# A DLRM tower on one core: gathers paced by the one two back, each with its own semaphore

## What is computed

```python
e = jnp.stack([tbl_0[ids[:, 0]], ..., tbl_25[ids[:, 25]]], axis=1)
combined = jnp.concatenate([dense_features[:, None, :], e], axis=1)        # 512 x 27 x 128
interactions = jnp.einsum('bfd,bgd->bfg', combined, combined)
z = jnp.concatenate([dense_features, interactions[:, iu, ju]], axis=1)    # iu, ju: upper triangle
h = jnp.concatenate([z, dense_features], axis=1)                          # 607 columns
h = jnp.maximum(h @ W_top1 + b_top1, 0.0)                                 # 512
h = jnp.maximum(h @ W_top2 + b_top2, 0.0)                                 # 256
y = h @ W_top3                                                            # 512 x 1
```

## Time and profile before

| | us |
|---|---|
| median of 3 runs | 160.23 |
| lowest and highest run | 157.64 and 160.42 |
| the profiled execution's own time | 156.5 |
| its span, from the first to the last instruction | 154.7 |

### The profile page before, as it was taken

One profiled execution on the slowest core, in us unless ns is written; L12 is line 12 of the kernel. 1 busy time (PEld: TensorE's weight loads), 2 busy tenths in 40 slices (PEclk: granted clock), 3 DMA queues, 4 the chain that ended last, 5 costly groups with the idle time before them and its releaser, 6 DMA issues.

```text
span 154.7 us, 2685 instructions
## 1 busy us (share of the span) xinstructions
PE 117.9 (76%) x1038; PEld 98.9 (64%) x1038; DVE 74.1 (48%) x153; ACT 73.0 (47%) x160; POOL 68.4 (44%) x75
## 2 busy tenths in 40 slices
PE   0689999985979967550595728489929989799994
PEld 0446776662756856540394628478829989798993
DVE  3499999999999960407204510030505020237000
ACT  6795994995897820426104522002505313236211
POOL 2648072260345747474447465446456474100000
PEclk9999999999999999776559997865985799999999
DMA  5828765487961011111112121111121111100000
GB/s 156 222 71 267 207 190 110 160 221 199 354 181 42 17 51 38 34 51 34 39 44 52 28 63 32 49 34 38 34 51 33 39 50 25 27 6 0 4 0 1
DMA packets 6304, 12.58 MB, mean 81 GB/s; under 512 B 2545, under 2 KB 3157, under 8 KB 6163
## 3 DMA queue, kind: packets, MB, share of 16 engines
q1 hardware_dynamic: 3971, 7.68, 17.2%
q0 software_dynamic: 2176, 4.46, 10.9%
q10 hardware_dynamic: 144, 0.26, 0.8%
HBM read 11.27 MB, written 0.00 MB: 73 GB/s over the span
## 4 chain that ended last, share of the span: by engine, by line
DMA 34%; PE 27%; POOL 24%; issue 13%; DVE 1%; ACT 1%
DMA rows<-in_tbl_dram,ids_i 31%; POOL rows L343 24%; PE ps L603 12%; PE ps L574 7%; PE ps L525 2%; PE ps L616 2%; DMA ids_i<-in_ids_dram 2%; PE ps L558 2%; DVE z L488 1%; PE ps L626 1%; PE ps L624 1%; ACT emb_t L403 0%; DVE h_t L497 0%; ACT y L430 0%
## 5 line engine op out<-in xcount | busy, mean ns | idle before, releaser
L343 POOL DMA_INDIRECT rows<-in_tbl_dram,ids_i x68 | 67.6, 994 | 63.0 <-DMA rows<-in_tbl_dram,ids_i 45.2
L461 DVE TENSOR_SCALAR hot<-ps,row_no 125x512 fp32r<-125x512 f32 x54 | 36.6, 739 | 1.0 <-PE ps L512 1.0
L488 DVE COPY z<-ps 32x112 f32<-32x112 f32 (+1 forms) x64 | 16.5, 258 | 34.9 <-PE ps L574 22.7
L574 PE MATMUL ps<-emb_t 128*64 128x52 f32 x512 | 23.6, 251 | 11.8 <-issue 8.3
L574 PEld LDWEIGHTS ps<-emb_t 128*64 128x64 f32 x512 | 21.1, 166 | 14.8 <-issue 11.3
L542 PE MATMUL ps<-hot,tab_hi 125*128 125x512 f32 x72 | 30.0, 416 | 0.8 <-issue 0.8
L411 ACT COPY z<-ps 32x112 f32<-32x112 f32 (+1 forms) x64 | 15.2, 238 | 30.8 <-PE ps L574 19.7
L545 PE MATMUL ps<-hot,tab_lo 125*128 125x512 f32 x72 | 29.1, 404 | 0.7 <-DVE tab_lo L450 0.7
L558 PE MATMUL ps<-ident,rows 128*128 128x128 f32 x68 | 12.0, 304 | 15.2 <-DMA rows<-in_tbl_dram,ids_i 9.7
L558 PEld LDWEIGHTS ps<-ident,rows 128*128 128x128 f32 x68 | 8.3, 153 | 18.3 <-DMA rows<-in_tbl_dram,ids_i 11.7
L542 PEld LDWEIGHTS ps<-hot,tab_hi 125*128 125x128 f32 x72 | 14.1, 196 | 5.5 <-issue 2.4
(11 more groups left out here) (44 smaller groups left out, 92.7 us busy)
## 6 DMA issues: line engine op xcount, KB each, us to landing
tab<-in_tbl_dram SPq DMA_DIRECT2D x9, 448.0 KB
rows<-in_tbl_dram,ids_i POOLq DMA_INDIRECT x68, 4.6
w_fold<-w_pair SPq DMA_DIRECT2D x1, 1024.0 KB
w<-in_W_top_dram SPq DMA_DIRECT2D x1, 512.0 KB, 5.1
tab<-in_tbl_dram SPq DMA_DIRECT2D x9, 52.0 KB
x_rows<-in_r_dense_features_dram ACTq DMA_DIRECT2D x1, 256.0 KB, 3.2
w_x<-in_W_top_dram SPq DMA_DIRECT2D x1, 256.0 KB
h_t<-in_W_top_dram SPq DMA_DIRECT2D x1, 256.0 KB
```

The costliest lines, as they stand in the source:

```text
L343: pool.indirect_dma_start(out=rows[:, t, gathered.index(f), :], out_offset=None, in_=tables[f - 1], in_offset=bass.IndirectOffsetOnAxis(id ...
L461: nc.vector.tensor_scalar(hot[0:RP, k % OHB], ps[0:RP, IDV + n % 2, :], row_no[0:RP, c:c + 1], None, ALU.is_equal).then_inc(hot_dve, 1)
L488: last = nc.vector.tensor_copy(dst, src)
L574: last = nc.tensor.matmul(ps[32 * q:32 * (q + GT), bank, col:col + GC], emb_t[:, t, b0:b0 + GT, :].rearrange("p b f -> p (b f)"), emb_t[:, ...
```

## The change

POOL no longer waits for a whole group ahead of the next. From the third gather on, each gather waits for the one two back, so that at most two are under way at any time. Each of the 68 gathers gets a semaphore of its own (before there were 20, one per group). PE's transposes wait for the gather that each of them reads, in place of one wait for the group ahead of the first. The wait for the PSUM bank stands ahead of them as before. Nothing else changes: the same 68 gathers in the same order, the same `ORDER`.

```diff
-        rows_in = [[sem(f"rows_in{t}_{g}") for g in range(NG)] for t in range(T)]
+        rows_in = [[sem(f"rows_in{t}_{f}") for f in gathered] for t in range(T)]
...
             pool.wait_ge(ids_in, 16)
+            fetched = []
             for t in range(T):
-                for g, group in enumerate(GROUPS):
-                    fetched = [f for f in features(group) if f]
-                    for n, f in enumerate(fetched):
-
-                        if n == 0 and g:
-                            pool.wait_ge(rows_in[t][g - 1], 16 * sum(a > 0 for a in features(GROUPS[g - 1])))
-                        elif n == 0 and t:
-                            pool.wait_ge(rows_in[t - 1][NG - 1], 16 * len(features(GROUPS[NG - 1])))
-                        pool.indirect_dma_start(
-                            out=rows[:, t, gathered.index(f), :], out_offset=None, in_=tables[f - 1],
-                            in_offset=bass.IndirectOffsetOnAxis(ids_i[:, t, f - 1:f], 0),
-                        ).then_inc(rows_in[t][g], 16)
+                for group in GROUPS:
+                    for f in features(group):
+                        if f:
+
+                            if len(fetched) >= 2:
+                                pool.wait_ge(fetched[-2], 16)
+                            landed = rows_in[t][gathered.index(f)]
+                            pool.indirect_dma_start(
+                                out=rows[:, t, gathered.index(f), :], out_offset=None, in_=tables[f - 1],
+                                in_offset=bass.IndirectOffsetOnAxis(ids_i[:, t, f - 1:f], 0),
+                            ).then_inc(landed, 16)
+                            fetched.append(landed)
...
-                    pe.wait_ge(rows_in[t][g], 16 * (len(feats) - (0 in feats)))
                     wait_bank(s)
                     for m, f in enumerate(feats):
+                        if f:
+                            pe.wait_ge(rows_in[t][gathered.index(f)], 16)
```

## The result

The changed kernel took 148.46 us (median of 4 runs, 146.66 to 151.37) against 158.95 us (median of 4, 157.64 to 160.42) for the kernel before, which has one run more here than in the table ahead (160.23): a ratio of 0.938, 95% interval 0.922 to 0.954. It is faster, by some 10 us; 151.4 was forecast, which is 150.1 when the 8.85 us are taken from 158.95. The profiled execution took 146.66 us with a span of 144.9, against 156.5 and 154.7 before, so 9.8 us of span are to be explained.

The account below looks back on a forecast made before the run. Gathers were taken to bound the kernel up to 104.02 us, PE the last 50.7. Removing PE's four waits (6.85) plus 2 us extra gave 8.85 off 160.2, so 151.4 us; range 146 to 158.

Parts of the forecast that it names:

- the likeliest case: Whole kernel: the forecast itself, a gain of 5.5 to 11 us, chance 0.58.
- The pace without loads: POOL's gathers in tiles 1 and 2: 1.40 us each, 34 in 49.8 us with slow rows, before 60.04.
- The pace beside loads: POOL's gathers up to 44 us, beside table loads: 2.33 to 3.00 us each with two under way, before 2.43.
- I take 43.4, in effect no change: Tile 0, beside table loads: the 17th gather lands at 43.4 us, before 43.94.
- Rival A: Table loads hold up the early gathers, the 17th landing at 48.7: time 156 to 158 us, chance 0.15.
- PE becomes the bound, with 3.5 us in hand: After the hot phase, at g4:2: PE reaches it at 97.2 us, its gather is due at 93.7.
- I take 2 us: PE's path: extra gain if low clock, gram stalls and late copies shrink, up to 3.5 us before g4:2.
- the late copies: DVE's copies of tile 0's second half began only at 70.49; PE waited 5.51 us before g3:1.
- the term for PE's four waits: Tiles 1 and 2: PE's waits for gathers at g4:1, g2:2, g3:2 and g4:2 all go, 6.85 us.
- B: Second half of the gram: PE's stalls last while gathers flow, 8.4 us more; 162 us, chance 0.08.
- C: Stalls and low clock, made by bunches of four gathers and by idling, go: 147 us, chance 0.12.
- D: Whole kernel: gain partly eaten by A and B, within 2%, 157 to 163 us, chance 0.07.

Follow-up runs that it names:

- e8: The changed kernel itself, run again beside other kernels on another chip: 151.84 us, ratio 0.958 to the kernel before.
- e1: Changed kernel, but POOL waits for whole groups in tile 0 and for the gather two back from tile 1 on: 147.59 us, ratio 0.916 to before.
- e2: Changed kernel, but POOL waits two back only in tile 0 and for whole groups from tile 1 on: 168.92 us, ratio 1.066 to before.
- e3: Changed kernel, but POOL waits for whole groups everywhere, each gather keeping its own semaphore: 167.18 us, ratio 1.050 to before.
- e5: Changed kernel, but a group's first gather waits only for the last gather of the group before: 158.63 us, ratio 0.993 to before.
- e6: As e5, but PE waits for all gathers of a group ahead of its first transpose: 158.26 us, ratio 0.993 to before.
- e9: Changed kernel, but gathers wait four back in tile 0 and two back from tile 1 on: 167.33 us against 156.2 for before.
- e12: Kernel before, with its shared group semaphores, but POOL waits for the group two back: 195.62 us, ratio 1.257 to before.
- e4: Changed kernel, but each gather waits for the one three back: 130.96 us, ratio 0.824 to before.
- e7: Changed kernel, but each gather waits for the one four back: 125.86 us, ratio 0.797 to before.
- e11: Changed kernel, but each gather waits for the one eight back: 200.71 us.
- e10: Changed kernel, but gathers wait two back in tile 0 and four back from tile 1 on: 188.8 us, ratio 1.207 to before.

## Why the prediction was right in its number, and where it wasn't in its reasons

The forecast was a gain of 8.85 us for the profiled execution; it was 9.8. The verdict, the range and the likeliest case held. Three of its steps did not, and they offset each other. In its own terms and on PE's path: 7.9 us were lost up to the gram where nothing was put; PE's waits for gathers grew by 0.4 us where 6.85 were to go; and the rest gave 18.2 us where 2 were put. That makes 9.9 in place of 8.85, so the number was right in part by luck.

**The pace without loads: right.** 34 gathers in 49.8 us were forecast for tiles 1 and 2; from 48.7 to 99.9 they took 51.2. From 60.30 to 63.06 is 2.76 us for two, against the 2.80 taken from the earlier trace rows. The remaining 1.4 us are single slow landings like the one ahead of 80.22. The Trainium skill, "DMA: Bandwidth & Descriptors", section "Anatomy of one DMA — SWDGE (gpsimd) path", gives a fixed cost and a rate by which one gather would take an estimated 2.15 us, less than the 2.50 us that POOL needs for two. The rows do not agree: they show 2.5 us from start to landing and 0.26 us of wake-up, and two back does bind.

**The pace beside loads: wrong.** The step that failed is "I take 43.4, in effect no change": the 17th landed at 48.7, past the 47 that the prediction itself named as its limit. The value was worked out from the cheap end, 4.39 us, for a pair; the rows show 4.12 to 6.98 us. Term by term, the fourth gather started at 9.81 in place of 8.7, the 13 after it came 2.80 us apart in place of 2.33, and only the last landing, 2.5 in place of 4.39, was cheaper: 48.7 in place of 43.4. Rival A named this mechanism and its middle value, 48.7, to the tenth. In PE's terms it cost 7.9 us: 4.8 in longer waits for gathers (2.9 to 7.7 us before the gram) and 3.5 in busy time at a lower clock (0.95 for 1.00), less some small waits that went. e8 repeats it and e1 and e2 place it in tile 0: with groups there the gram starts at 57.1 to 60.3 (before, e1, e3, e5, e6), with two back at 65.3 to 66.7 (changed, e2, e8).

**"PE becomes the bound, with 3.5 us in hand": wrong.** The gathers bind to the end, and PE still waits 7.2 us for them. I had read the block of six transposes with no idle time ahead at 133.62 as proof that PE bounds the last 50 us. It was close to a tie: the last gather landed some 0.1 us before the block began and, by an estimate from the block's 0.82 us, some half a microsecond before its own two transposes, the last of the six. A row without idle time shows that the other side wasn't later, not that it had slack; for that its own landing must be read. e5 makes the tie visible: PE's stalls taken away, the gathers left at before's pace, and the time is the same, since both limits lay side by side. The table sets the start of the last gather beside the span, for the kernels in which the engines do not stand for long (e9 to e12 are left out):

| kernel | last gather starts | span | difference |
|---|---|---|---|
| before | 130.99 | 154.7 | 23.7 |
| changed | 121.69 | 144.9 | 23.2 |
| e1 | 120.80 | 146.5 | 25.7 |
| e2 | 142.10 | 166.8 | 24.7 |
| e3 | 140.24 | 165.6 | 25.4 |
| e4 | 105.37 | 130.0 | 24.6 |
| e5 | 130.98 | 156.1 | 25.1 |
| e6 | 129.97 | 155.7 | 25.7 |
| e7 | 96.41 | 123.0 | 26.6 |
| e8 | 125.55 | 150.2 | 24.7 |

In the changed kernel, e1, e2, e3, e5, e6 and e8 the chain that ended last runs over the gathers up to the last one or the last but one. In before (up to 103.98), e4 (up to 86.8) and e7 (no gather) it does not, and there the similar difference doesn't mean that gathers set the time: PE has much the same work left behind its last transposes in every kernel.

For the changed kernel, where they do, the sum is short: the last gather came 9.3 us sooner, 4.8 lost early and 14.1 won later.

**"I take 2 us" on top of the waits: too small.** The stalls (8.0), the late copies (3.5) and the clock (6.7) gave PE 18.2 us, not 2. That is what let PE follow gathers which came 9.3 us sooner at their end, after it had started its gram 7.9 us later. With the 2 us forecast it could not have. So the mechanism was right and this term undersized, while the term for PE's four waits, 6.85 us, did not come at all: they were replaced by ten shorter ones.

**The rivals.** A's cause was right and its time, 156 to 158, wrong, for it left the later gain at 6.85 + 2. B did not occur: "issue" fell to 0.3 us where it should have grown by 8.4. But engines that stand beside a stream of gathers, as it feared, are seen in e9 to e12. C came nearest in time (147): that the stalls would go came true, but not its reason, that bunches of four had made them, since e5 and e6 keep the bunches and have no stalls. D is excluded by the interval.

**Open: what makes the engines stand.** It isn't the wait of PE (e6), it needs no shared semaphore (e9 to e11), and an uninterrupted stream of gathers doesn't bring it by itself (e7 over 50 us, e10 from 46 to 65). It outlasts the stream, by 8 us in e10 and 12 in e11. Nor is it known whether the 8.3 us of the kernel before are the same thing on a smaller scale. A run of e7 or e8 on the chip of the last set, or of e10 on another, would tell program from chip; it wasn't made.

## What to carry to other kernels

Where a queue of short transfers is throttled by "wait for the one k back", compare the landing time with what k issues take: two back still bound at 2.5 us of landing against 1.25 us per issue, three and four back gave 0.824 and 0.797 of the time, and the longest landings, beside bulk loads, count. Find what binds by the landing of the last item on each side, not by the absence of idle time in one row. A deeper stream must be measured on more than one chip before it is adopted: kernels of the same kind took 126 us and 189 us here, and whether program or chip made the difference is open.

## What the runs showed of the hardware that I had not expected

- A gather beside table loads lands after 4.1 to 7.0 us in the changed kernel's chain (the first after 3.7), without them mostly after 2.5. Twice as many under way did not make it twice as long: the gather that waits for it started 4.4 to 7.2 us after it with two under way, 6.1 to 7.9 with four (e7).
- Several waits ahead of one instruction on GpSimd cost more than one, but not by their number: 2.40 us of pause with four waits and 2.44 with two (e3), against 1.89 with one (e5). Why is open.
- PE, DVE and ACT can stand for 26 us and more while GpSimd issues indirect DMAs without a pause, with matmuls coming one per 2.80 us (e10), and for up to 12 us beyond (e11); at other times they work beside it undisturbed (e7).
